# Source gathers of a pair in two runs of twelve, each released by one tile of look-ups, in a graph-layer kernel

## The reference

```
h   = maximum(layernorm(x), 0)
e   = concat(h[src], h[dst], edge_attr)          # one row of 96 for each edge
v   = relu(e @ W1 + b1) @ W2 + b2                # 96 -> 64 -> 32
m   = segment_max(v, dst, 12500)
out = x + maximum(m, h)
```

## Time and profile before

| what | us |
|---|---|
| median of three runs | 3181.32 |
| profiled execution, its span | 4798.8 |
| TensorE matmuls busy in it | 3796.5 |
| GpSimd busy in it | 2386.6 |
| gathers of h, 2269, mean 947 ns | 2147.7 |

### The profile page before, as it was taken

The page is one execution under the profiler, slowest core; times in us unless marked ns, Lnnn a source line. Parts: engine busy times, 40 slices in busy tenths (PEclk is TensorE's granted clock), DMA queues, the critical chain, the costliest instruction groups (busy, mean ns, idle before and its releaser), DMA issues.

```text
span 4798.8 us, 56874 instructions
## 1 busy us (share of the span) xinstructions
PE 3796.5 (79%) x19778; PEld 2547.3 (53%) x19778; DVE 2178.1 (45%) x2474; ACT 2192.4 (46%) x2555; POOL 2386.6 (50%) x2523
## 2 busy tenths in 40 slices
PE   5858788778878877877887788778877887778787
PEld 3536455555555545555555555555555555555465
DVE  4211554445444444544444455444444454445356
ACT  2214454445444444544444445444544454445355
POOL 6653455555455455455545555555455555554310
PEclk8979888888778888888887888888888888888798
DMA  8700222222222222222222222222222222222112
GB/s 255 279 10 25 70 80 88 92 85 61 57 68 63 56 66 69 56 61 68 68 55 63 68 65 61 60 69 68 56 63 68 69 61 56 68 68 68 46 55 56
DMA packets 200553, 350.32 MB, mean 73 GB/s; under 512 B 73791, under 2 KB 124251, under 8 KB 200117
## 3 DMA queue, kind: packets, MB, share of 16 engines
q1 hardware_dynamic: 116638, 303.65, 18.4%
q0 software_dynamic: 80448, 41.33, 6.2%
q10 hardware_dynamic: 3332, 4.01, 0.3%
HBM read 240.36 MB, written 119.78 MB: 75 GB/s over the span
## 4 chain that ended last, share of the span: by engine, by line
PE 60%; issue 19%; another core or an unknown queue 10%; DVE 8%; ACT 2%; DMA 0%; DVEq 0%; ACTq 0%; SPq 0%
PE ps_rows L938 38%; PE ps_layers L968 8%; PE ps_layers L963 5%; DVE onehot L1250 3%; PE ps_layers L918 2%; PE ps_layers L953 2%; PE ps_layers L912 2%; DVE max_t L1318 2%; PE ps_layers L957 2%; PE ps_layers L1006 1%; DVE src_t L1285 1%; DVE rows_in L1323 1%; ACT onehot L852 0%; DVE dst_t L1305 0%
## 5 line engine op out<-in xcount | busy, mean ns | idle before, releaser
L664 POOL DMA_INDIRECT src_in<-h_dram,src_ix x2269 | 2147.7, 947 | 1951.5 <-PE ps_rows L938 976.5
L938 PE MATMUL ps_rows<-onehot,table 128*128 128x512 f32 x9898 | 2553.2, 418 | 109.0 <-issue 89.3
L938 PEld LDWEIGHTS ps_rows<-onehot,table 128*128 128x128 f32 x9898 | 1986.6, 203 | 728.8 <-issue 292.8
L852 ACT ACTIVATE onehot<-distance 128x1024 fp32r<-128x1024 bf16 x909 | 905.0, 1049 | 855.0 <-PE ps_rows L938 607.3
L847 ACT ACTIVATE distance<-picks,below_column 128x1024 bf16<-128x1024 int16 x909 | 985.1, 1139 | 0.7 <-DMA picks<-picks_dram 0.7
L838 ACT ACTIVATE hid<-ps_layers,b_col 128x512 f32<-128x512 f32 (+1 forms) x404 | 241.6, 680 | 1407.9 <-remote 912.0
L1300 DVE STREAM_TRANSPOSE ps_layers<-rows_in 128x512 f32<-128x512 f32 x202 | 133.3, 706 | 1561.3 <-ACT hid L838 1561.2
L968 PE MATMUL ps_layers<-picked_rows,w_src 128*64 128x128 f32 x1552 | 399.9, 390 | 550.1 <-issue 545.7
L1250 DVE SCALAR_TENSOR_TENSOR onehot<-picks,column,ps_layers 128x1024 fp32r<-128x1024 int16 x404 | 499.8, 1258 | 310.2 <-PE ps_rows L938 164.7
L968 PEld LDWEIGHTS ps_layers<-picked_rows,w_src 128*64 128x64 f32 x1552 | 188.8, 180 | 784.9 <-issue 782.2
L1318 DVE TENSOR_TENSOR_SCAN max_t<-mask_in,max_t,ps_layers 128x512 f32<-128x512 bf16 x196 | 249.0, 1271 | 337.2 <-remote 331.4
(11 more groups left out here) (145 smaller groups left out, 1283.1 us busy)
## 6 DMA issues: line engine op xcount, KB each, us to landing
picks<-picks_dram SPq DMA_DIRECT2D x101, 512.0 KB
first_rows<-hid SPq DMA_DIRECT2D x100, 500.0 KB
rows_in<-in_edge_attr_dram SPq DMA_DIRECT2D x96, 512.0 KB
rows_in<-first_rows SPq DMA_DIRECT2D x96, 512.0 KB
run_max<-rows_in SPq DMA_DIRECT2D x96, 512.0 KB
src_in<-h_dram,src_ix POOLq DMA_INDIRECT x2269
mask_in<-mask_dram SPq DMA_DIRECT2D x96, 256.0 KB
h_dram<-h_sb ACTq DMA_DIRECT2D x4, 392.0 KB, 5.9
```

The source lines that it names most:

```text
L664: pool.indirect_dma_start(out=src_in[:, slot, g, r, :], out_offset=None, in_=rows[:, :], in_offset=bass.IndirectOffsetOnAxis(ap=src_ix[:, ...
L852: nc.scalar.activation(onehot[:, RING_AT[c] + BY_DVE[c] + k, :, :].rearrange("p g w -> p (g w)"), distance[:, k, :], ACT.Relu, bias=1.0, s ...
L938: mm = nc.tensor.matmul(ps_rows[g][side][:, 0:WIDE], table[:, i * SIDES + side, part, :], onehot[:, RING_AT[c] + t, g, :], start=(i + part ...
```

## The change

The twelve bursts of a pair become two runs, one for each group. The first run waits until one tile of the look-ups that follow layer one of pair p - 7 is done (`tiles_before` is now 13 (p - 5), with `RUN_AT` 1), the second until seven are. Each run has 12 gathers with nothing between them; the short pair's second run has one. The constant `SLACK` and its shift of six tiles are gone. The first gathers (pairs 0 to 6), the scatters, the gathers of the maxima and the lists of all other engines are as they were.

```diff
@@ -77,7 +77,7 @@
 PARTS = 2
 
 BURST = 2
-SLACK = 6
+RUN_AT = [1, 7]
 BURSTS = 2 * GATHERS // BURST
 assert GATHERS % BURST == 0
 assert BURSTS * BURST == 2 * GATHERS
@@ -679,13 +679,11 @@
 
 
             def gather_pair(half, slot, tiles_before, short=False):
-                for b in range(BURSTS // 2 + 1 if short else BURSTS):
-                    pool.wait_ge(tiles_used, tiles_before + b)
+                for g in range(2):
+                    pool.wait_ge(tiles_used, tiles_before + RUN_AT[g])
                     pool.sem_inc(gathers_begun, 1)
-                    if short and b == BURSTS // 2:
-                        gather_row(half, slot, 1, 0)
-                    else:
-                        gather_burst(half, slot, b)
+                    for r in range(1 if short and g else GATHERS):
+                        gather_row(half, slot, g, r)
 
 
             def gather_turn(turn, half, loads, last=False):
@@ -694,7 +692,7 @@
                 for slot in range(AHEAD - last):
                     pool.wait_ge(src_turned, turn * (2 * AHEAD) + (slot * 2 + 2 - 2 * AHEAD))
                     pool.sem_inc(gathers_begun, 1)
-                    gather_pair(half, slot, turn * (AHEAD * TILES) + (slot + 2 - AHEAD) * TILES - SLACK, last and slot == AHEAD - 2)
+                    gather_pair(half, slot, turn * (AHEAD * TILES) + (slot + 2 - AHEAD) * TILES, last and slot == AHEAD - 2)
 
             pool.wait_ge(first_ix_loaded, A * D)
             gather_early(0)
```

## The result

The kernel before takes 3181.7 us (median of four runs, 3181.28 to 3184.22), the changed one 3196.73 (four runs, 3195.63 to 3199.28). The ratio is 1.0048, 95% interval 1.0035 to 1.006: the change costs some 15 us, where the forecast was 13 (3194, own range 3188 to 3200).

What follows compares the result with a forecast made beforehand. The prediction took GpSimd's back-to-back issue of gathers as the bound: 3181.3 us measured before, 0 for the pitch, plus 13 for the later first release, made 3194 us. Own range 3188 to 3200; 8 in 10 range 3170 to 3206.

Steps and rivals of the forecast that it cites:

- The bound: GpSimd's issue of 2514 indirect DMAs at 1.2508 us bounds the timed runs; back to back they sum to 3162 us.
- The pitch: Time between gathers on GpSimd: removing some 900 semaphore waits changes nothing, bounds -2 to +2 us, taken as 0.
- the 1% that was named: Sign in the changed kernel's profile: GpSimd's busy time of line L664 stays unchanged within 1%.
- The release: Pair 7's first gather now waits for a tile behind layer one of pair 0; lasting delay taken as 13 us.
- the bounds of 10.9 and 18.9: Lasting delay of GpSimd: low end the distance of one pair's two releases (5.4 + 5.46), high end 18.9 us.
- The other case: Pair 7, if the scatters decided its old start (E + 7.5): GpSimd stands 11.5 to 16.8 us longer.
- layer one of pair 0 at E + 13.5: Set-up: with E the scatters' end, the `first_rows` load and 6.40 us of VectorE put layer one at E + 13.5.
- GpSimd late at the last stored pair by 14 us: At the end: GpSimd gets there 114 us after pair 96's last gather, TensorE and the stores some 100 after it.
- second rival: No change, 3181 us: pitch under 1.137 us with lead enough, or delay taken up at the end; chance 0.16.
- the lead: TensorE starts some 191 us of gathers ahead, loses 2.7 us each pair and waits for gathers in the last third.
- Faster: First rival: TensorE bounds, and gathers moved out of layer one give back time, 3140 us; chance 0.12.
- a slowdown by VectorE: Third rival: gathers moved beside other VectorE work take longer, 0 to 533 us, by one estimate 3207 us; chance 0.03.

Runs made afterwards that it cites:

- second trace of the same kernel: The kernel before, no edit, traced once more (also called second trace of before): one run 3182.07 us, its profiled execution 3180.2 us.
- early runs of twelve: The changed kernel with RUN_AT = [-6, 0], two runs of twelve released where the first and seventh burst were before: 3184.03 us, ratio 1.0007.
- the last kernel: The kernel before with slot-emptying transposes earlier in VectorE's list in the first fourteen pairs, and SLACK = 19: 3177.5 us, ratio 0.9988.
- the dose: The changed kernel with RUN_AT = [14, 20], releases one pair's 13 tiles later: 3221.47 us, ratio 1.0128 against the kernel before.
- extra_matmuls: The kernel before with half of layer one's edge matmuls done twice (eight more a pair): 3215.34 us, ratio 1.0103.
- few_matmuls: The kernel before with a quarter of layer one's edge matmuls done twice (four more a pair): 3211.37 us, ratio 1.0077.

## Why the prediction was right

**The bound held.** GpSimd's list sets the end: ninety more DMAs of 1.206 us cost 106.8, and 42.1 us more of waiting at its head cost 39. Setting aside the stalls of the first trace, and keeping only its durations, is what made the sum possible; the second trace of the same kernel shows none of them. The changed kernel's own timed runs also lie on the sum of the prediction: 3162 + 26.0 + 5.9 = 3194, with 3196.7 measured.

**The pitch held.** In runs of twelve, gathers start 1.249 us apart, and the early runs of twelve equal the bursts of two. Line L664's busy time differs by 0.1%, inside the 1% that was named.

**The release held, by another road.** The forecast had two cases for pair 7, with 13.6 to 18.9 us if the slot and not the scatters decided before. The slot decided; the releases are 373.22 - 357.16 = 16.1 us apart. Pair 8 gives back 1.94 (0 to 3 forecast). 14.94 lies in the bounds of 10.9 and 18.9; I took 13, near the low end, for a giving-back that turned out smaller. The other case, 11.5 to 16.8 if the scatters decided, holds 14.94 by luck alone: it rests on the step that failed next.

**Failed: layer one of pair 0 at E + 13.5.** The scatters end at 340 us, and layer one starts at 364.73, E + 25. The rows around it, changed kernel:

```profile
338.66 0.96 POOL L711 DMA_INDIRECT first_rows<-h_sb,scatter_ix  x1 [0.30 <-issue]
...
348.27 1.28 DVE L1248 SCALAR_TENSOR_TENSOR onehot<-picks,column,ps_layers 128x1024 fp32r<-128x1024 int16 x1 [4.16 <-PE ps_rows L936]
...
355.10 1.56 DVE L1283 STREAM_TRANSPOSE src_t<-src_in 128x384 f32<-128x384 f32 x2
...
364.73 2.01 PE L951 MATMUL ps_layers<-ea_t,w_edge 32*64 32x512 f32 x16 [6.98 <-DVE onehot L1248]
```

The step counted the load of `first_rows` and VectorE's work behind it, read from a trace in which the scatters came so late that everything else was done. In an undisturbed run VectorE comes to this work late: its one-hots for pair 1 wait for look-up tiles until 348.27, and the rest of its set-up stands behind them, up to the transposes of slot 0 at 355.10. Both releases hang on those transposes, and VectorE's work between them and layer one did not change: their end lies 8.1 us ahead of layer one in the earlier trace rows, in the second trace of before (356.20 and 364.27) and in the changed kernel. So the error fell out of the difference.

**Failed: GpSimd late at the last stored pair by 14 us.** It is early, by 3.82 us before and 5.89 after. The step counted the some 100 us of TensorE and the stores from pair 96's last gather; layer one of pair 96 starts 23 us after that gather (3065.51 against 3042.20, second trace of before). By the prediction's own second rival all of the delay should then have vanished. It did not, since the last pairs themselves wait for the last gathers: layer one of pair 96 starts 15.1 us later in the changed kernel (3080.65), and the wait at the end even grew by 2.07. The prediction's main line had said so ("TensorE waits for the last of them"); its second rival left it out. A wait at the end absorbs a delay only if what is waited for does not hang on the delayed engine.

**Mis-sized: the lead.** "GpSimd falls 2.7 us further behind each pair" is wrong for pairs 4 to 13, where TensorE takes 30.5 us itself, and TensorE's 80 to 100 us below the measured time were some 41. The gates stay as close as they were for that long: 0.94 us at 731.92 with slot 0 free, 5.48 at 805.88 in the last kernel. In the changed kernel the margin was enough, and none was waited for.

**The rivals.** Faster needed a pitch under 1.137 us and starved layer ones; neither is there. No change needed the delay taken up in the lead or at the end; the dose says no. Of a slowdown by VectorE there is no sign in the loop: the gathers' line in the changed kernel (duration ns, min, median, max; first and last start) against the earlier trace rows, all of them and then those from 346 us on:

```profile
L664 POOL DMA_INDIRECT src_in<-h_dram,src_ix x2269: 940/944/1575, 69.3 to 3055.4; - x190
...
L664 POOL DMA_INDIRECT src_in<-h_dram,src_ix x2150: 940/944/962, 346.2 to 3055.4; - x196
```

The median is 944 with the runs beside look-ups, 945 in the second trace of before, and behind the set-up none takes over 962. The long ones lie in the set-up, and there VectorE does hold GpSimd up (timeline, changed kernel):

```profile
37.79 0.99 DVE L1111 TENSOR_SCALAR mask<-mask 125x3200 bf16<-125x3200 bf16 x1
...
37.92 1.68 POOL L664 DMA_INDIRECT src_in<-in_x_dram,src_ix  x1 [0.31 <-issue]
```

This gather of x begins 0.13 us behind a `TENSOR_SCALAR` of 0.99 us and takes 1.68: 0.73 above the median, most of the 0.86 that were left of it. In the traces of all runs, 72 of GpSimd's indirect DMAs took more than 1.3 us. All of them are of the set-up, and each began beside one of two kinds of VectorE work: this `TENSOR_SCALAR` (13) or an instruction that reads two tiles from SBUF, the core's on-chip memory (59). The loop has neither, but for one instruction on three elements: there VectorE transposes, or reads one of its two tiles from PSUM, TensorE's result memory (`ps_` in the rows). The Trainium skill, "SBUF — State Buffer", section "Who interferes with whom", has GpSimd shut out for the length of a VectorE instruction in a two-port mode, and names `tensor_scalar` among the operations that can enter one. The trace agrees at the `TENSOR_SCALAR`, though its row does not name the mode; in the loop no run tests the rule.

## What to carry to other kernels

When an engine that issues back to back is the bound, count its idle time: a change costs what that grows by in all. Here one wait, at the head of the loop, held nearly all of it, and the shape of the later waits did not matter. A wait taken out of a ring comes back at the next gate, so follow the releases pair by pair (what is released when, against when the engine is free) until the engine is behind for good. And before any wait is read from a trace, compare its span with the timed runs; if it is half as long again, use the durations and have the kernel traced once more.

## What the runs showed of the hardware that was not expected

One traced execution of the kernel before took 4798.8 us and another 3180.2, with timed runs of 3181; the gathers' mean was 947 ns in one and 946 in the other. An indirect DMA of 128 rows occupied GpSimd for 945 ns, one of four rows for 894. Beside the loop's VectorE work an indirect DMA of GpSimd took 940 to 962 ns (2150 of them, changed kernel); beside some VectorE instructions of the set-up one took up to 2.78 us (extra_matmuls and few_matmuls). Doing four edge matmuls twice lengthened TensorE's pair by 0.82 us, doing eight twice by 0.83; why the two are alike was not tried.
